# Two batches a phase apart: one batch's MLPs and projections between the other's attention slots, and the value product in one piece

## Time and profile before

| | |
|---|---|
| median of 3 runs | 490.38 us (489.73 to 490.95) |
| the profiled execution | 488.39 us |
| its span, first to last instruction | 486.6 us |
| mean granted TensorE clock | 0.825 |
| TensorE busy | 317.5 us (65%) |
| VectorE busy | 303.9 us (62%) |
| ScalarE busy | 251.0 us (52%) |
| GpSimd busy | 121.9 us (25%) |

### The profile page before, as it was taken

One profiled execution on the slowest core, in us unless ns is written; L12 is line 12 of the kernel. 1 busy time (PEld: TensorE's weight loads), 2 busy tenths in 40 slices (PEclk: granted clock), 3 DMA queues, 4 the chain that ended last, 5 costly groups with the idle time before them and its releaser, 6 DMA issues.

```text
span 486.6 us, 6451 instructions
## 1 busy us (share of the span) xinstructions
PE 317.5 (65%) x2274; PEld 148.4 (31%) x2274; DVE 303.9 (62%) x683; ACT 251.0 (52%) x550; POOL 121.9 (25%) x184
## 2 busy tenths in 40 slices
PE   0015844621245563988988888758678977788786
PEld 0004613511103420222222345535222232333354
DVE  0778787759588659888888314346675354554230
ACT  3267645562466212788887773333435354456542
POOL 0112139640363510000000202563012222222410
PEclk9999965555557756799999999989757598889799
DMA  7940350000000233000000000000710000000001
GB/s 243 417 186 0 130 223 0 1 0 0 1 0 1 68 99 92 2 3 3 1 2 2 2 2 1 0 1 20 198 43 2 1 2 3 2 1 2 1 1 43
DMA packets 11652, 21.90 MB, mean 45 GB/s; under 512 B 2010, under 2 KB 10462, under 8 KB 10846
## 3 DMA queue, kind: packets, MB, share of 16 engines
q1 hardware_dynamic: 11620, 21.49, 12.8%
HBM read 14.54 MB, written 0.52 MB: 31 GB/s over the span
## 4 chain that ended last, share of the span: by engine, by line
PE 41%; DVE 24%; ACT 18%; POOL 6%; issue 6%; DMA 2%; SPq 2%; DVEq 0%; ACTq 0%; POOLq 0%
PE pe L1475 10%; ACT big L1173 8%; PE pe L1497 6%; DVE nm L932 5%; PE pe L1376 4%; PE pe L1529 4%; PE pe L1451 4%; PE pe L1454 3%; PE pe L1247 2%; POOL rstd L344 2%; ACT scr L1058 2%; PE pe L1341 2%; PE pe L1426 1%; DVE st L516 1%; DVE xn L526 1%
## 5 line engine op out<-in xcount | busy, mean ns | idle before, releaser
L1173 ACT ACTIVATE big<-pe 128x512 f32<-128x512 f32 (+3 forms) x256 | 116.7, 521 | 81.6 <-PE pe L1497 80.4
L932 DVE TENSOR_REDUCE nm<-pe 128x2 f32<-128x1024 f32 (+2 forms) x112 | 124.2, 1145 | 50.1 <-PE pe L1454 38.1
L1475 PE MATMUL pe<-big,scr 128*32 128x256 f32 (+4 forms) x896 | 74.1, 408 | 3.8 <-ACT scr L1146 2.6
L1451 PE MATMUL pe<-big 62*128 62x512 bf16 (+3 forms) x256 | 53.1, 395 | 15.9 <-DVE nm L932 13.0
L1497 PE MATMUL pe<-big 64*128 64x512 bf16 (+3 forms) x256 | 54.9, 371 | 8.4 <-ACT big L1173 7.0
L344 POOL TENSOR_TENSOR rstd<-var,half 128x4 f32<-128x4 f32 x26 | 28.5, 1097 | 110.5 <-DVE var L521 85.9
L440 POOL TENSOR_SCALAR_AFFINE_SELECT big<-big 128x512 f32<-128x512 f32 x32 | 20.3, 635 | 73.4 <-ACT big L1173 73.4
L1497 PEld LDWEIGHTS pe<-big 64*128 64x128 bf16 x256 | 15.7, 94 | 64.7 <-ACT big L1173 33.5
L430 POOL CAST nm<-nm 128x16 bf16<-128x16 f32 x16 | 3.1, 196 | 102.0 <-DVE nm L932 102.0
L526 DVE TENSOR_SCALAR xn<-x_tok,mv,rstd 128x128 f32<-128x128 f32 x64 | 18.6, 353 | 15.7 <-POOL rstd L344 15.7
L1475 PEld LDWEIGHTS pe<-big,scr 128*32 128x32 f32 x896 | 18.9, 111 | 29.2 <-issue 12.3
(11 more groups left out here) (188 smaller groups left out, 560.3 us busy)
## 6 DMA issues: line engine op xcount, KB each, us to landing
big<-tern SPq DMA_DIRECT2D x48, 128.0 KB, 2.4
big<-in_fill SPq DMA_DIRECT2D x1, 4096.0 KB, 13.6
big<-in_wa SPq DMA_DIRECT2D x1, 2304.0 KB, 12.5
w<-in_w SPq DMA_DIRECT2D x2, 1152.0 KB, 19.2
big<-in_wa SPq DMA_DIRECT2D x1, 1344.0 KB, 6.2
big<-in_w SPq DMA_DIRECT2D x1, 1024.0 KB, 14.4
w<-in_w SPq DMA_DIRECT2D x1, 896.0 KB, 19.8
rowg<-in_rowg SPq DMA_DIRECT2D x1, 832.0 KB, 18.4
```

The costliest lines, as they stand in the source:

```text
L932: v.tensor_reduce(dst, src[:, :, 0:w * len(pairs)].rearrange("p r (h w) -> p r h w", w=w), AX.X, ALU.max, negate=True).then_inc(sem(f"a{a} ...
L1173: s_.activation(P[:, kt % PRING, 2 * p + j, q0:S], bank[SINGLES[i % 3]][:, q0:S], ACT.Exp, scale=SCALE).then_inc(sem(f"a{a}_p"), 1)
L1451: last = t_.matmul(dsts[par][:, k * wd:(k + 1) * wd], QZ[rows, b, 2 * g + i, qt * 128:(qt + 1) * 128], KZ[rows, b, 2 * g + i, 0:wd], start ...
L1475: last = t_.matmul(bank[PV_BANK][32 * h:32 * h + 32, lo:hi], V[b][:, kt, HG * g + h, :], P[:, k % PRING, h, lo:hi], start=(kt == 0), stop= ...
```

## The change

- `schedule`, `SEQ` and the loops over the parts go. One list `ORDER` (from `work_order`) holds every event of both attentions and all MLPs in order; every engine walks through it and does its share of each event. The ring of two PSUM pairs goes on through all of it, and the MLPs' products, turns and the second attention's queries, keys and values go through the ring too.
- Batch 0's parts 1, 2, 3 stand in the slots 43 to 63 of the first attention, which are exponentials of batch 1. Batch 0's part of the second attention begins right after (`GAP`). Batch 1's part 1 stands between the first maxima of the second attention (`BEFORE`), its parts 2 and 3 and its queries, keys and values in the slots 0 to 26 (exponentials of batch 0), and its maxima begin in slot 27 (`GATE`). Batch 0's last MLP stands in the slots 43 to 48, batch 1's follows the last slot (`TAIL`).
- `table` calls between attention and MLPs go, but for the one ahead of the first exponential: where a function of another table comes, the compiler puts a load ahead of it.
- The value product of a key tile is whole (all its columns in one piece, each second slot), not in halves; the copy of a unit's result follows its last product. More maxima stand ahead of the first slot (13 for 12; 10 for 9), and the parts stand behind the second maximum of the next unit or three slots after the pieces.
- The masked bias of part 2 is multiplied once by GpSimd before the first attention, into `row0`, and added in one instruction.
- Semaphores are counted through instead of one set for each attention.

The core of the diff (the same events on each engine are left out):

```diff
-                    for s in range(64):
-                        u, kt, p = s // 8, s // 2 % 4, s % 2
...
-                        for x in slots[s + 1]:
-                            ring_item(*x)
-                        if s >= LATE[causal]:
-                            probs_out((s - LATE[causal]) // 2, (s - LATE[causal]) % 2)
...
+        AHEAD, LAG, LATE, GATE = (13, 10), 2, (3, 5), 27
...
+        def mlp(n, b, at):
+
+            ins = [("in", n, b, c) for c in range(0, MLPS[n]["n"], 2)]
+            return {at: [("xn", n, b)], at + 1: [("turn", n, b)], at + 2: [("bias", n, b)], at + 3: ins,
+                    at + 4: [("res", n, b)], at + 5: [("res2", n, b), ("add", n, b)]}
...
+        SIDE = (placed(projected(0, 0, 38), {41: [("root", 1, 0)]}, mlp(1, 0, 43), {49: [("root", 2, 0)]},
+                       mlp(2, 0, 51), {57: [("root", 3, 0)]}, {59: [("xn", 3, 0)], 60: [("turn", 3, 0)],
+                       61: [("bias", 3, 0), ("in", 3, 0, 0)], 62: [("res", 3, 0)], 63: [("res2", 3, 0), ("add", 3, 0)]}),
+                placed({0: [("res", 1, 1)], 1: [("res2", 1, 1), ("add", 1, 1)], 2: [("root", 2, 1)]},
+                       mlp(2, 1, 4), {11: [("root", 3, 1)]}, mlp(3, 1, 12), {19: [("root", 4, 1)]},
+                       {21: [("xn", 4, 1)], 22: [("turn", 4, 1)], 23: [("bias", 4, 1), ("qk", 1, 1)],
+                        24: [("stack", 1, 1, 0), ("less", 1, 1), ("v", 1, 1)], 25: [("mid", 1, 1), ("vals", 1, 1)],
+                        26: [("low", 1, 1), ("stack", 1, 1, 1), ("stack", 1, 1, 2)]},
+                       projected(4, 0, 38), {41: [("root", 5, 0)]}, mlp(5, 0, 43)))
...
+            def consumed(e):
+
+                i = STARTED.index(e)
+                if i >= len(RING):
+                    name, count = taken(STARTED[i - len(RING)])
+                    pe.wait_ge(sem(name), count)
+                return bank[PLACE[e]], bank[PLACE[e] + 1]
...
                 for h in range(HG):
-                            last = t_.matmul(bank[PV_BANK][32 * h:32 * h + 32, lo:hi], V[b][:, kt, HG * g + h, :],
-                                             P[:, k % PRING, h, lo:hi], start=(kt == 0), stop=(kt == TB - 1 and part == 1),
-                                             tile_position=(0, 32 * h))
+                    last = t_.matmul(bank[PV_BANK][32 * h:32 * h + 32, q0:S], V[b][:, kt, HG * g + h, :],
+                                     P[:, k % PRING, h, q0:S], start=(kt == 0), stop=(kt == TB - 1),
+                                     tile_position=(0, 32 * h))
...
+                elif kind == "in":
+                    n, b, c0 = e
                     m = MLPS[n]
...
+                    act.wait_ge(sem("ring"), MADE["in", n, b, c0])
+                    for c in range(c0, c0 + 2):
+                        s_.activation(hid[:, b, c], bank[PLACE["in", n, b, c0] + c - c0], m["func"],
+                                      bias=col[:, m["bias"] + c:m["bias"] + c + 1]).then_inc(sem(f"hid{b}"), 1)
```

More of the change, by code:

```diff
@@ L276, in ring_place @@
[L276 to L280 removed]
+        STEPS = (max_steps(False), max_steps(True))
+        AHEAD, LAG, LATE, GATE = (13, 10), 2, (3, 5), 27
+        TURN_BANK, QK_BANKS, V_BANKS = 4, (2, 3, 4, 2), (5, 3)
+        RING, SINGLES, PV_BANK = (0, 6), (2, 3, 4), 5
+        HIDDENS = {n: sum(MLPS[k]["n"] for k in MLPS if k < n) for n in MLPS}
@@ new lines, in maxima_rows @@
+            def maxima_rows(a, u):
+                b, g = u // 4, u % 4
+                sp.wait_ge(sem("nmp"), 8 * a + u + 1)
+                for par in range(2):
+                    at = HALF * par + KROWS
+                    sp.dma_start(QZ[at:at + 2, b, 2 * g:2 * g + 2, :],
+                                 nmp[16 * par:16 * par + 16, u % 2]).then_inc(sem(f"mrow{u % 2}"), 16)
+            for b in range(B):
+                for part in range(3):
+                    stack(0, b, part)
+            for kind, *e in ORDER:
+                if kind == "stack":
+                    stack(*e)
+                elif kind == "parts":
+                    maxima_rows(*e)
+                elif kind == "add" and e[0] == 5:
+                    b = e[1]
+                    sp.wait_ge(sem(f"x{b}"), 6)
+                    sp.dma_start(out[b].rearrange("(t p) d -> p t d", p=128), x_tok[:, bt(b)]).then_inc(sem("stored"), 16)
@@ new lines, in _ @@
+            for k in range(B):
+                nc.gpsimd.memset(V[k][:, :, :, 8:16], 1.0).then_inc(sem("v_ready"), 1)
+            n_root(0, 1)
+            add_bias(0, 1)
+            for t in range(B * TB):
+                link(nc.gpsimd.tensor_scalar(mask_bias[:, t], gate_bias(2, t // TB), maskf[:, t:t + 1], None, ALU.mult))
+            for kind, *e in ORDER:
+                if kind == "pieces":
+                    maxima_parts(*e)
+                elif kind == "triangle":
+                    lower_triangle(*e)
+                elif kind == "root":
+                    n_root(*e)
+                elif kind == "bias":
+                    add_bias(*e)
@@ new lines, in _ @@
+            for kind, *e in ORDER:
+                if kind == "max":
+                    maxima(*e)
+                elif kind == "parts":
+                    maxima_turned(*e)
+                elif kind == "out":
+                    unit_normalised(*e)
+                elif kind == "add":
+                    residual(*e)
+                elif kind == "xn":
+                    n_normed(*e)
+                elif kind == "less":
+                    a, b = e
+                    dve.wait_ge(sem("ring"), MADE["qk", a, b])
+                    for qk in range(2):
+                        less_high(a, b, qk, bank[PLACE["qk", a, b] + qk])
+                elif kind == "low":
+                    low(*e, 0)
+                    low(*e, 1)
+                elif kind == "vals":
+                    a, b = e
+                    dve.wait_ge(sem("ring"), MADE["v", a, b])
+                    values(a, b, bank[PLACE["v", a, b]])
+                elif kind == "q1_less":
+                    less_high(0, 1, 0, bank[QK_BANKS[2]])
+                elif kind == "q1_low":
+                    low(0, 1, 0)
+                    less_high(0, 1, 1, bank[QK_BANKS[3]])
+                elif kind == "k1_low":
+                    low(0, 1, 1)
+                    value_0(1)
@@ new lines, in exponentials @@
+            def exponentials(a, s):
+                u, kt, p = s // 8, s // 2 % TB, s % 2
+                q0 = 128 * kt if a else 0
+                k = 32 * a + s // 2
+                if p == 0 and k >= PRING:
+                    act.wait_ge(sem("pv"), k - PRING + 1)
+                for j in range(2):
+                    i = 128 * a + 2 * s + j
+                    act.wait_ge(sem("sc"), i + 1)
+                    s_.activation(P[:, kt % PRING, 2 * p + j, q0:S], bank[SINGLES[i % 3]][:, q0:S], ACT.Exp,
+                                  scale=SCALE).then_inc(sem("p"), 1)
```

783 lines of the change are left out of this document (350 added, 433 removed).

## The result

The kernel after the change takes **519.06 us** in the median (518.9 to 519.12, 4 runs), the kernel before, beside it, 490.06 us (489.27 to 490.95, 4 runs). The ratio is 1.0591, 95% interval 1.0571 to 1.061: slower by 5.9%. Predicted were 498 us and a range of 479 to 511. The side was right, the size wasn't: 29 us were lost, not 7.5. The profiled execution took 518.90 us, its span is 517.1.

The account below looks back on a forecast made before the run. Three engines near their limits bound the first attention, a chain with no engine full the middle; first attention +21, middle -43, first maxima +10.5, second attention +19, tail 0 gave +7.5 us, 497.9 us as a median, range 479 to 511.

Parts of the forecast that it names:

- three MLP places: Batch 0's MLPs in first attention slots 43 to 63: 10 + 7 + 7 us, less 2 for slots without maxima.
- 38.1: Second attention: us added by batch 1's MLP work, turn, products, values and stack stop, and batch 0's last MLP.
- 101 - 16.5 - 3 + 38.1: Second attention: today's 101 us, -16.5 for shorter units, -3 for slots without maxima, +38.1 for added work.
- 27.4 us (3.8 + 14 + 3.6 + 6): Second attention, batch 1: wide product out 3.8, narrow MLPs 14, turn, products and values 3.6, stack stop 6.
- 6 us stands: Second attention, slot 27: TensorE's queue stands 6 us for batch 1's stack, and with it slot 28's scores.
- Rival B: Much slower: stops at loads and stack drop TensorE to the lower level, 13 us more, 511 us; chance 0.11.
- a gain of 0.6 us a unit, a loss of 0.1 us a slot pair: Bounds for the whole value product in place of two halves, in the first attention.
- 10.8 us: First attention's unit with the whole product: VectorE's 9.9 us plus 0.9 us without its next block of scores.
- sits behind the wait and isn't hidden: ScalarE's table load starts only when its activation's wait ends; 11 more loads are 14 us of ScalarE.
- the 2.5 us at each place: Hole at each MLP in the slots, where TensorE waits for load and GELUs: between 0 and 2.7 us, 2.5 taken.
- rival D: A drain ahead of each load, as a queue on ScalarE: at most 9 us over 11 loads, 507 us; chance 0.03.
- Rival A: Faster: engines fill some 17 of 27 us of holes between TensorE and ScalarE, 481 us; chance 0.30.
- Rival C: The middle shrinks and the slots pay all of it, within 1.5 us of 490.4 us; chance 0.09.

Follow-up runs that it names:

- e4: The kernel before with only the masked bias multiplied once, ahead of the first attention, and added in one instruction: 483.79 us.
- e7: The changed kernel with batch 1's MLPs, queries, keys, values and stack done ahead of the second attention's first maxima: 524.70 us.
- e5: The changed kernel with batch 0's last MLP moved from slots 43 to 48 of the second attention to behind its last slot: 516.16 us.
- e6: The changed kernel with batch 0's three MLPs taken out of the first attention's slots and done one after the other behind it: 538.32 us.
- e1: The changed kernel with each value product again in two halves and a unit's copy one slot later: 511.32 us.
- e2: The kernel before with only the value product made whole, in the slot of its first half: 497.36 us.
- e3: The changed kernel with Identity in place of both GELUs, so no table load behind the one for the exponential: 516.03 us.
- e8: The kernel before with the masked bias multiplied once and GpSimd splitting a unit's maxima as soon as the last is there: 471.23 us.
- e12: The kernel of e8 with the value product whole in the second attention and its parts behind the next unit's second maximum: 479.90 us.

## Why the prediction was wrong, point by point

**Right.** That the middle is one batch's chain of 21 us (20.2), that the first maxima take 22, that the tail doesn't gain, that the masked bias is covered by GpSimd (e4). A bare unit of the second attention: 10.2 us forecast, 10.1 in e7. The last MLP there: 10.7 forecast, 11.4 measured (e5). The three MLP places in the first attention: 22 forecast, 19.8 measured (e6).

**The step that failed, second attention, "38.1".** The sum for this stage was 101 - 16.5 - 3 + 38.1 = 119.6 us; it took 137.2, 17.6 more. The largest part is batch 1's work, put at 27.4 us (3.8 + 14 + 3.6 + 6). It cost 39.1: the first five units take 99.3 us with it and 60.2 without (table of e7). The first two of them cost 19.9 us against 3.8 + 14 = 17.8, a difference within the scatter of the second (16.4 to 19.3 us). The two around the stack cost 19.3 against 9.6. So 9.7 of the 17.6 us missed are that the stack was costed as its stop ("6 us stands") and not as what follows it: the lower clock until about 428, and a whole unit's maxima in a row. 0.7 is the last MLP. The other 5.2 are the bare stage, 86.7 us against 81.5, although its middle units are as forecast; where in it they lie was not taken apart. Rival B named the mechanism (stops drop TensorE to the lower level) at 13 us and with 0.11; it was close in kind and was not added to the forecast, where at the stack it belonged. How the 9.7 divide between the clock and the maxima in a row was not measured; by the windows above the maxima have the larger part.

**The whole product, "a gain of 0.6 us a unit, a loss of 0.1 us a slot pair".** Wrong in sign. I had compared sums (1.6 us of TensorE against 1.6 of exponentials in hand). The three score banks don't let TensorE run ahead that far: the pair costs 2.67 us. The measured loss is 7.7 us in the kernel after (e1) and 7.3 in the kernel before (e2). "10.8 us" a unit was 12.0. Together with the cheaper MLP places it makes the first attention 114.9 instead of 111.

**The load that "sits behind the wait and isn't hidden".** Wrong. The 11 added loads were put at 14 us of ScalarE, inside the 2.5 us at each place. The row at 340.15 shows the load ahead of the wait, and all 15 are worth 3 us in the median (e3). The first maxima, in which the load at 352.02 does follow a wait, fell by 1.8 us there. The Trainium skill, "ScalarE: Activation LUTs", section "What ACT_TABLE_LOAD costs", states 2.66 us for a switch with its drain. Here GELU ends at 276.14, the load runs from 276.16 to 277.44 and the exponential starts at 277.45: no drain, so rival D is out.

**Rival A** (holes filled, faster) is out: loads are covered, but the holes at the stack and at the score banks are not. **Rival C** would have needed 490 us.

**Where the expected gain went.** A batch's MLPs cost 41 us alone (e6) and 20 in slots, and that looks like a bargain. But in the kernel before two batches' MLPs already cover each other: 63.8 us hold the three MLPs of both, the norm, the products and the stack. What is measured against is not 41 + 41. The middle is 43.6 us shorter, of which about 5 come from the masked bias alone (e4), and the slots and maxima ask 71.7. The change also holds two gains that don't need it, the bias and the early pieces. The kernel before with just these takes 471.2 us (e8), so the rest of the change costs 48 us, some 8 of them by the whole product and some 40 (an estimate by difference) by the moved work with its new order.

## What to carry to other kernels

Before work is moved into the gaps of a full stage, ask what it costs where it is: two chains side by side are already half hidden. Cost a stop on TensorE with what follows it (the lower clock and the work that has piled up), and a product's form by how far the banks let TensorE run ahead, not by mean loads. Test the small edits of a large change one by one: here a masked bias multiplied once and one GpSimd step placed earlier give 471 us, 4% under the kernel before and 9% under the kernel after.

## What the runs showed of the hardware that was not expected

- A table load (1.28 us) can be issued ahead of the wait of its activation (340.15 against 345.32) and right behind an operation, with no drain. The load at 352.02 came behind a wait of 1.01 us and the first load of the kernel behind one of 4.29 us; what decides was not followed up.
- A pause of about 1 us in TensorE costs 0.6 to 1.1 us when the granted clock stays at 1.00 behind it, and 2.0 to 2.9 us when it falls: 0.95 us at the parts (e8), 1.16 us at the output's turn (e12). The same pause has both outcomes within one execution. The kernel after is at the lower level in the slots without maxima too, where TensorE is busy 6.68 of 8 us at 0.50:

```profile
478.00:486.00 8.00, 6.68 (x37) 1.35 (x36) 0.00 (x0) 5.42 (x15) 1.91 (x3) 0.50 0.00 0
```

- The mean granted clock of an execution doesn't tell its time: the runs of the kernel after have 0.897 and 0.802 at 518.9 and 519.05 us. Why it differs was not followed up.
